# A graph layer on one core: slot one-hots laid out with the tiles innermost, and the weights read from them at a step

## What is computed

```
h = jnp.maximum(_layernorm(x, axis=-1), 0.0)          # x: 6250 nodes x 64
h_src = h[src]                                        # 200000 edges, sorted by dst
for r in range(16):
    msg = msg + h_src * (etypes == r)[:, None] @ weight[r]      # weight: 16 x 64 x 64
out = x + jax.ops.segment_sum(msg, dst, num_segments=6250)
```

## Time and profile before

| | |
|---|---|
| median of three runs | 1200.71 us (1197.76 to 1206.26) |
| profiled execution, span from first to last instruction | 1203.7 us |
| PE busy | 1083.9 us, 90% |
| DVE busy | 938.3 us, 78% |
| POOL busy | 682.1 us, 57% |
| ACT busy | 450.0 us, 37% |
| mean granted clock of PE, whole span | 0.984 |

### The profile page before, as it was taken

How to read it: one execution, slowest core, us unless ns; L and a number is a source line. 1 busy time by engine, 2 the same in 40 slices (tenths; PEclk the granted TensorE clock), 3 DMA queues, 4 the chain that set the end, 5 groups by cost and what they waited for, 6 DMA issues and landing times.

```text
span 1203.7 us, 39145 instructions
## 1 busy us (share of the span) xinstructions
PE 1083.9 (90%) x15421; PEld 740.5 (62%) x15421; DVE 938.3 (78%) x2773; ACT 450.0 (37%) x1157; POOL 682.1 (57%) x647
## 2 busy tenths in 40 slices
PE   3998999899989889999999999999999999999897
PEld 1445666666666566666666666666666666666665
DVE  7756878897877688788778778878887887888874
ACT  4884333333333333333333333333333333333332
POOL 2213665566666665667666666666665656666630
PEclk9998999999999899999999999999999999999999
DMA  6795222222222122222222122222222222222211
GB/s 173 301 401 186 59 61 59 58 59 59 62 59 59 37 57 59 59 60 58 59 58 57 43 59 58 60 59 58 60 59 60 59 58 59 58 60 59 59 32 56
DMA packets 41739, 93.69 MB, mean 78 GB/s; under 512 B 14572, under 2 KB 14574, under 8 KB 41557
## 3 DMA queue, kind: packets, MB, share of 16 engines
q1 hardware_dynamic: 13850, 42.12, 10.3%
q0 software_dynamic: 19776, 20.29, 9.9%
q10 hardware_dynamic: 7930, 28.76, 6.2%
HBM read 63.52 MB, written 27.59 MB: 76 GB/s over the span
## 4 chain that ended last, share of the span: by engine, by line
PE 74%; issue 8%; DVE 6%; ACT 5%; another core or an unknown queue 3%; DMA 2%; ACTq 1%; POOL 0%; SPq 0%; DVEq 0%; POOLq 0%
PE ps L1281 33%; PE ps L1264 21%; PE ps L1308 6%; PE ps L1324 3%; ACT u L602 3%; PE ps L1173 3%; DVE u L946 2%; PE ps L1164 2%; PE ps L1197 2%; DMA table<-u 1%; DMA w_cat<-weight 1%; PE ps L1158 1%; PE ps L1203 1%; PE ps L1186 1%
## 5 line engine op out<-in xcount | busy, mean ns | idle before, releaser
L529 POOL DMA_INDIRECT u<-table,row_idx x583 | 612.7, 1051 | 411.3 <-PE ps L1264 138.8
L1281 PE MATMUL ps<-u 64*64 64x512 bf16 (+1 forms) x7280 | 466.5, 377 | 18.0 <-issue 16.0
L672 ACT CAST u<-ps 128x384 bf16<-128x384 f32 (+1 forms) x630 | 265.2, 465 | 527.8 <-PE ps L1264 464.2
L946 DVE TENSOR_SCALAR u<-iota_key,z_sb 128x512 bf16<-128x512 f16 x1190 | 359.9, 368 | 70.3 <-PE ps L1281 50.9
L1264 PE MATMUL ps<-parts,u 128*128 128x192 bf16 x3430 | 333.6, 250 | 11.0 <-issue 9.3
L1281 PEld LDWEIGHTS ps<-u 64*64 64x64 bf16 x7280 | 215.0, 106 | 204.7 <-issue 75.9
L1264 PEld LDWEIGHTS ps<-parts,u 128*128 128x128 bf16 x3430 | 280.6, 99 | 41.0 <-issue 38.5
L936 DVE TENSOR_SCALAR u<-u,node_id 128x1152 bf16<-128x1152 f16 (+2 forms) x420 | 184.5, 495 | 0.0
L681 ACT COPY u<-ps 128x512 f32<-128x512 f32 x140 | 75.2, 589 | 109.5 <-remote 76.8
L966 DVE TENSOR_TENSOR accT<-accT,ps 128x32 f32 x238 | 44.8, 188 | 58.4 <-DVE accT L966 23.1
L1308 PE MATMUL ps<-u,w_cat 128*64 128x128 f32 x1120 | 77.4, 277 | 1.7 <-ACT u L681 1.2
(11 more groups left out here) (131 smaller groups left out, 656.4 us busy)
## 6 DMA issues: line engine op xcount, KB each, us to landing
u<-rel_dram SPq DMA_DIRECT2D x70, 544.0 KB
table<-u ACTq DMA_DIRECT2D x24, 1024.0 KB, 5.2
u<-table,row_idx POOLq DMA_INDIRECT x583
rel_dram<-rel_row SPq DMA_DIRECT2D x70, 4.2 KB
x_sb<-x SPq DMA_DIRECT2D x2, 448.0 KB
out<-h_sb SPq DMA_DIRECT2D x3, 224.0 KB
out<-h_sb ACTq DMA_DIRECT2D x3, 224.0 KB
msg_x<-table,spill_row POOLq DMA_INDIRECT x35
```

Source lines behind the costliest of these rows:

```text
L529: pool.indirect_dma_start(out=msg_p[:, b, j, :], out_offset=None, in_=table, in_offset=bass.IndirectOffsetOnAxis(ap=row_idx[:, j, m:m + 1] ...
L672: act.copy(msg_s[:, u % MB, 0:width, :].rearrange("p q c -> p (q c)"), ps[gather_bank(u)][:, 0:width * ROW]).then_inc(s_gev, 1)
L946: dve.tensor_scalar(khot[:, v % KR, :], iota_key[:, :], z_sb[:, n % 3, 1, q:q + 1], None, ALU.is_equal).then_inc(s_khot, 1)
L1281: last = pe.matmul(ps[3 + a][half * D:(half + 1) * D, keys], msg_s[rows, u % MB, q % 2, part * D:(part + 1) * D], khot[rows, v % KR, keys] ...
```

## The change

The slots' one-hots get the other order in memory. Before, a tile's places lay side by side (`p j z`: tile j outermost); now the seven tiles of one place lie side by side (`p z j`, the tile innermost). So that every operand of `placed` steps by one element, the places 0 to 64 are written out once, each seven times (`iota_place`, 455 elements, one more `iota` of POOL at the start), and `rank` and `spill_rank` are kept in 16 bits in place of 32. PE now takes the 128 (or 64) weights of a tile at a step of seven elements, 14 bytes.

```diff
-        rank = sb("rank", [P, PT])
+        rank = sb("rank", [P, PT], F16)
-        spill_rank = sb("spill_rank", [P, NPR, PT])
-        spill_hot = sb("spill_hot", [P, SJ, 2 * XC], F16)
+        spill_rank = sb("spill_rank", [P, NPR, PT], F16)
+        spill_hot = sb("spill_hot", [P, 2 * XC, SJ], F16)
+        iota_place = sb("iota_place", [P, (CAP + 1) * SJ], F16)
...
-        slot_hot = u2[:, a0:a0 + PT * CAP // 2].bitcast(F16).rearrange("p (j z) -> p j z", j=SJ)
+        slot_hot = u2[:, a0:a0 + PT * CAP // 2].bitcast(F16).rearrange("p (z j) -> p z j", j=SJ)
...
-            for tile, pattern, base, per in ((iota_range, [[1, SQ]], 0, 0), (iota_slot, [[1, P]], 0, 0),
+            for tile, pattern, base, per in ((iota_range, [[1, SQ]], 0, 0), (iota_slot, [[1, P]], 0, 0), (iota_place, [[1, CAP + 1], [0, SJ]], 0, 0),
...
-            pool.wait_ge(s_const, 8)
+            pool.wait_ge(s_const, 9)
...
             def placed(hots, first, ranks, n):
-                there = hots[:, :, :].rearrange("p j (a z) -> p a j z", a=2)
-                places = iota_slot[:, first:first + n].rearrange("p (a j z) -> p a j z", a=1, j=1).to_broadcast([P, 2, SJ, n])
-                mine = ranks.rearrange("p (a j z) -> p a j z", j=SJ, z=1).to_broadcast([P, 2, SJ, n])
+                there = hots[:, :, :].rearrange("p (a z) j -> p a z j", a=2)
+                places = iota_place[:, first * SJ:(first + n) * SJ].rearrange("p (a z j) -> p a z j", a=1, j=SJ).to_broadcast([P, 2, n, SJ])
+                mine = ranks.rearrange("p (a z j) -> p a z j", a=2, z=1).to_broadcast([P, 2, n, SJ])
                 return dve.tensor_tensor(there, places, mine, ALU.is_equal)
...
-                    last = pe.matmul(ps[6][:, 0:4 * SQ].rearrange("p (a c) -> p a c", a=2), slot_hot[:, j, :], values[:, :, j, :],
+                    last = pe.matmul(ps[6][:, 0:4 * SQ].rearrange("p (a c) -> p a c", a=2), slot_hot[:, :, j], values[:, :, j, :],
...
-                    last = pe.matmul(ps[6][at:at + 2 * XC, 480:488].rearrange("p (a v) -> p a v", a=2), spill_hot[:, j, :],
+                    last = pe.matmul(ps[6][at:at + 2 * XC, 480:488].rearrange("p (a v) -> p a v", a=2), spill_hot[:, :, j],
```

More of the change, by code:

```diff
@@ L798, in sort_ranges @@
                 if g == 0:
-                    dve.wait_ge(s_const, 8)
+                    dve.wait_ge(s_const, 9)
                     dve.wait_ge(s_turned_s, 2)
@@ L819, in sort_slots @@
                                        ALU.mult))
-                step(dve.tensor_reduce(rank[:, :], ranks[:, :, :], AX, ALU.add))
+                with nc.allow_low_precision(reason="one term of each sum is not zero, a whole number below 2048"):
+                    step(dve.tensor_reduce(rank[:, :], ranks[:, :, :], AX, ALU.add))
                 if g >= 1:
@@ L1151, in sort_ranks @@
                     pe.wait_ge(s_turned_s, 6)
-                    pe.wait_ge(s_const, 8)
+                    pe.wait_ge(s_const, 9)
                 pe.wait_ge(s_ranges, g + 1)
```

## The result

The changed kernel takes 1204.95 us (median; 1201.26 to 1213.22), the kernel before beside it 1201.31 us (1197.15 to 1208.40). The ratio is 1.0031, with a 95% interval of 1.0015 to 1.0046: slower by 3.7 us where I had forecast 10. That is the result on this chip. On another chip, further down, the same two kernels stand at 1.0212. The profiled execution of the changed kernel was the longest of its 22 (1213.22 us, span 1211.5), so a difference of some us between the two traces is not yet one between the kernels. That its span lies 2 us from the 1213.7 us of the forecast is chance.

A forecast was written before the change was run, and what follows sets the result against it. PE was taken to bound the long stage, DVE's savings helping only where PE waits for it. 1203.7 - 10 (DVE's relief) + 20 (PE's loads) = 1213.7 us profiled, 1211 us on the 1200.7 median; range 1190 to 1256.

The forecast's parts named there:

- DVE's saving: The two one-hot comparisons on DVE reach two elements per cycle, saving 697 ns a pair, 48.8 us in all.
- Rival 3: DVE's comparisons stay at one element per cycle, so the 10 us are not gained: 1221 us; chance 0.08.
- What the saving is worth: DVE's relief ahead of the permutation: 9 us of PE's waits plus 1 us for one avoided slow-clock stretch, 10 us gained.
- 20 waits by 0.465 us: PE's waits for DVE before the permutation each shrink by the slots' saving: 9.3 us at most, taken as 9.
- Rival 4: DVE's relief is worth all its waits and more, 19.1 + 3 us, beside 20 us of cost: 1199 us; chance 0.06.
- The load of 64 columns: PE's weight loads for the spilled edges' seven products: 38 ns more each at the step, 0.26 us a pair.
- Rival 1: The step is free on PE, so the 20 us fall away: 1191 us, down to 1184; chance 0.20.
- The load of 128 columns: PE's weight loads for the slots' permutation: 19 ns more each, mostly hidden, 0.04 us a pair, side-by-side loading kept.
- rival 2: The permutation's 128-column load loses side-by-side form: 0.95 us a pair in all, 1256 us; chance 0.24.
- nearly its full length: In the long stage, 100 to 1190 us, work added to PE is paid almost whole: 0.30 us a pair, 20 us.
- The iota: The added 455-element operation on POOL at the start is hidden by an idle of 12.26 us; uncovered, under 1 us.

The follow-up runs named there:

- micro: The changed kernel with a bench added at its end: weight loads at several steps and comparisons cut into rows of different length; no kernel time given.
- slot_relief: Kernel before with only the slots' one-hots in the new layout and PE reading 128 columns side by side (wrong permutation, same work); ratio 0.9995.
- pairs: Kernel before, old layout, each rank written twice in 16 bits by a copy ahead of each comparison, giving rows of two; ratio 1.0004.
- pairs_again: The kernel of pairs, unaltered, against the kernel before on another chip (1196.63 us); ratio 1.0013.
- relief_again: The kernel of slot_relief, unaltered, against the kernel before on a chip where that takes 1066.02 us; ratio 0.9872.
- before_again: The kernel before, unaltered, run once for a second trace, on a chip where the kernel before takes 1196.63 us.
- after_again: The changed kernel, unaltered, against the kernel before on a chip where that takes 1066.02 us; ratio 1.0212.
- stride_again: The kernel of stride_only, unaltered, against the kernel before on a chip where that takes 1066.02 us; ratio 1.0272.
- stride_only: The changed kernel with ranks kept in 32 bits: DVE at its old times, PE still reading at the step; ratio 1.0006 to the kernel before.
- delay: Kernel before with three unused products of 392 moving columns put ahead of the spilled edges' seven in each pair; ratio 1.0051.
- spill_only: Kernel before with only the spilled edges' one-hots in the new layout, the slots' in the old; ratio 1.0021.
- spill_again: The kernel of spill_only, unaltered, against the kernel before on another chip (1196.63 us); ratio 1.0027.
- few: Kernel before with one product instead of seven in the permutation and one instead of seven for the spilled edges (output wrong); ratio 0.9972.
- delay2: Kernel before with six unused products of 392 moving columns ahead of the spilled edges' seven in each pair; ratio 1.0445.
- tiny: Kernel before with nine products of 64 loaded and 8 moving columns ahead of the spilled edges' seven; ratio 1.0078.
- slot_again: Kernel before with only the slots' one-hots in the new layout, the spilled edges' in the old, on a chip at 1066.02 us; ratio 0.9972.

## Why the prediction was right or wrong

**Direction right, size wrong, and right for a reason that I did not have.** The forecast was -10 + 20 = +10 us; +3.7 was measured. Both terms were off, and the difference of the two hid it.

- *DVE's saving.* Forecast 627 and 395 ns, measured 692 and 428: 42 us, not 48.8. The rate was right, the rows of seven were not. 896 elements in rows of seven take 692 - 162 = 530 ns, which is 510 cycles of 1.04 ns, 128 rows at four cycles each. The seventh element of a row takes a cycle for itself. The section 5.1 of the Trainium skill (Vector Engine (DVE) Microarchitecture Reference) that I drew on, by which a pair may span two rows, does not hold for this instruction: 692 against 626 ns in micro. The 4-byte alignment of its page VectorE: DVE Perf Modes was not needed either: the spill's places begin at 14 bytes, and 428 ns is far from 627. Rival 3 is excluded.
- *What the saving is worth.* Forecast 10 us. On the chips that stall, slot_relief, pairs and pairs_again measure it at -2 to +1 us of gain: nothing. On the chip that does not, relief_again measures 14 us for the slots' part. So "20 waits by 0.465 us" failed as a step on the first kind. PE's waits for DVE ahead of the permutation are 9.0 us in the changed kernel, as forecast, and the end did not follow. How much they fell is uncertain: the 19.1 us that the term was read from are those of one trace, and before_again has 13.2. On the second kind 14 us are near the forecast's 10, but that is no proof of the count of waits, which was made in a trace with stalls. Rival 4 had 22 us for DVE's relief. In the changed kernel it is worth at most about 6 us, on the chip without stalls (after_again against stride_again), so rival 4 is excluded.
- *The load of 64 columns.* Forecast 38 ns more, 0.26 us a pair; measured 88 ns and 0.50 us. This is the mis-sized term: 0.59 ns a column came from a row of 128 columns of 4 bytes, whose load at step 1 already took 141 ns, and it is 1.37 ns for 64 columns of 2 bytes. Rival 1 is excluded.
- *The load of 128 columns.* Forecast 19 ns more, 0.04 us a pair, and the fast form kept; measured 57 ns and 0.16 to 0.18 us, and the form is kept. 153 ns is above the 130 ns that I had given as the point of rival 2, yet its 216 ns and 1.1 us did not come: the products follow at 53 to 56 ns, not 129. Rival 2 is excluded by that pace. The rule of the Trainium skill (TensorE: Matmul & The Clock Gate, weight-path perf modes), that the fast load may be strided, agrees with these runs.
- *PE's added time costs "nearly its full length".* The terms above put that time at 46 us. stride_only, delay, spill_only and spill_again, with 34 to 46 us added, cost 1 to 6 us. On the chip without stalls, stride_again pays 29 of the 46 us. This sentence of the forecast, read from PE busy for 92% of the long stage, is the step that failed most, and on both kinds. With the right size of the loads and this sentence, I would have forecast +36 us. The two errors, 26 us too little of work and some 40 us too high a price for it, nearly cancelled. That the forecast came within 7 us is luck.
- *The iota* cost nothing that can be seen: stride_only, which has it too, stands at 1.0006.

**Why PE's time was nearly free.** Of the 46 us, 18 come back in the sums right behind the spilled edges: from the first of them to the ranks, 2.44 us in the kernel before and 2.17 in the changed one on average, where the undisturbed 36 products take 2.07. This stretch holds in every trace of the stalling chips. It is 2.44 to 2.53 us in the six with at most 12 us added to PE, and 2.15 to 2.30 us in the six with 34 to 46 us added. The stretch ahead of the permutation also fell between the two traces, from 1.39 to 1.18 us, but that is not shown to be an effect of the change: in the other five traces with little or nothing added it is 1.21 to 1.22 us. The rest is spread over the other stretches. On the chips at 1066 us the sums take 2.07 us in every kernel, and there is nothing of that to come back. I call it shown that these stalls are there on three of the five chips and not on the other two, and that they shrink as work is added ahead of them. That this is what makes PE's time cheap is argued from sizes: 46 us cost 1 us with stalls and 29 without, a difference of 28, and the loads of the sums idle 19 to 27 us less in stride_only than in the traces without added work.

What the stalls are is not shown, but the kept traces narrow it. I counted the gaps of over 350 ns between the starts of two loads of one line, from 100 to 1190 us. The kernels with at most 12 us added to PE have 207 to 218 of them on the stalling chips, those with 34 to 46 us added 114 to 158, and no trace of the chips at 1066 us has more than 6. They are not scattered. Of the 209 in pairs, 153 stand within two loads of one in pairs_again, on another chip. Of the 218 in the kernel before, 115 do so in before_again, and only 4 to 20 if the count of loads of the one is shifted by 15 to 500. So a stall belongs to a place in the kernel's work, and not to a disturbance from outside at some moment.

Nor is it the transfer of PE's instructions. DMA queue 8 carries them, in packets of 16 KB: their number follows PE's count of instructions from run to run (126 in before, 119 in few, 129 in delay2, 130 in tiny). First before, then few (packets, MB, share of 16 engines):

```profile
q8 instruction: 126, 2.06, 0.7%
```
```profile
q8 instruction: 119, 1.95, 0.8%
```

A packet takes 958 ns at the median in before and 995 in before_again, and no less on the other kind, 1001 ns in few and 973 in after_again. 37 of the 215 gaps up to 1150 us overlap such a packet in before, and 27 to 43 do when the packets' times are shifted by 1 to 80 us: no more than chance. What is left open is what holds PE back at these places, and why on some chips only. That longer products give PE time to catch up would fit, but the test for it, tiny, ran on a chip without stalls.

**Which bound is the kernel's.** On a chip without stalls PE and DVE share it: +16, +46 and +74 us on PE cost 8, 29 and 47; -27 gives 3; -28 on DVE gives 14, or 26 when PE is relieved too. There the change is a clear loss of 2.1%, and the layout of the slots alone (slot_again, 0.3% faster) is the best of the versions run there that compute the whole layer. On the first kind it is even with the kernel before. The layout of pairs, which takes 24 us off DVE and adds nothing to PE, was not run on a chip without stalls; by relief_again's half it should gain more than slot_again, some 12 us, which is an estimate.

## What to carry to other kernels

A share of 92% does not make an engine's time full price: before adding its work up, look for idle time of its loads that nothing explains, since it can shrink as you add work. Read a wait from two traces before it becomes a term of a sum: PE's waits for DVE were 19.1 us in one trace of the kernel before and 13.2 in the other. A layout that is good for the engine that writes must be priced at the engine that reads, once for each load: here the spilled edges put 0.50 us on PE for 0.20 us off DVE, and the slots 0.17 us for 0.40. And two kernels may stand otherwise on another chip: 1.003 and 1.021 were the same two programs.

## What the runs showed of the hardware

- Weight loads at a step of 14 bytes, 16-bit columns: 64 columns 113 to 201 ns, 128 columns 96 to 153 ns; beyond 16 bytes the price hardly rises (64 columns, at a granted clock of 0.50: 217 to 222 ns from step 8 to 28). From product to product, 105 ns (in micro, clock 0.50) and 118 ns (in the kernel, 0.99) for 64 columns, and 53 and 56 ns for 128, so 128 columns are cheaper to load than 64. The Trainium skill has lines of 16 bytes (SBUF — State Buffer, the note on cachelines), and these runs agree in that the price ends there.
- DVE with two 16-bit sources at step 1: 626 ns for 896 elements in rows of 2 to 896, all even, and 692 ns in rows of seven.
- One program, five chips: 1066, 1066, 1178, 1197 and 1198 us, each with a granted clock of 0.99 in the mean of its executions. Stalls of PE with nothing awaited go with the longer times, stand at the same places on different chips, and do not coincide with the transfers of PE's instructions (37 of 215; 27 to 43 by chance). Whether it is the chip itself or something around it, these runs do not tell.
